# Six buffers for gathered rows in a mixture-of-experts decoder layer, with the projection weights split later

## What is computed

```python
logits = einsum('bsd,de->bse', x, router_w) + router_b
topk_vals, topk_idx = top_k(logits, 2)
topk_w = softmax(topk_vals)
h = einsum('td,edf->etf', x, expert_w) + expert_b
combined = sum over the two experts of topk_w * silu(h)
out = combined @ proj_w + proj_b
y = x + out
x = layernorm(x + norm_w * y / sqrt(mean(y*y) + eps))
```

## Time and profile before

| | |
|---|---|
| median of 3 runs | 1613.41 us (1609.93 to 1615.18) |
| profiled execution | 1619.38 us, span 1617.6 us |
| PE busy | 1476.6 us, 91% |
| DVE, ACT, POOL busy | 963.2, 654.9, 647.8 us |
| mean granted TensorE clock | 0.961 |
| end of cross attention, start of the expert stage's matmuls | about 1394 and 1419 us from the span's start |
| last expert matmul, last instruction | about 1532 and 1617 us |

### The profile page before, as it was taken

How to read it: one execution, slowest core, us unless ns; L and a number is a source line. 1 busy time by engine, 2 the same in 40 slices (tenths; PEclk the granted TensorE clock), 3 DMA queues, 4 the chain that set the end, 5 groups by cost and what they waited for, 6 DMA issues and landing times. The chain is left out here.

```text
span 1617.6 us, 27685 instructions
## 1 busy us (share of the span) xinstructions
PE 1476.6 (91%) x8462; PEld 1208.2 (75%) x8462; DVE 963.2 (60%) x3585; ACT 654.9 (40%) x1763; POOL 647.8 (40%) x1003
## 2 busy tenths in 40 slices
PE   6999999999997589999999999999999999389876
PEld 6777877878865377888888888878888888277754
DVE  3666566566665375566655665556555665744467
ACT  4434344343341263444444443444444446333344
POOL 1334334234232254344444444343443444354173
PEclk8999999999998789999999999999999999789988
DMA  6221221221211532111111212111121113565472
GB/s 204 103 73 61 91 71 61 91 71 61 92 61 52 175 121 69 52 60 58 42 59 54 63 39 62 59 54 53 42 67 50 61 47 109 195 171 158 136 224 82
DMA packets 60957, 139.75 MB, mean 86 GB/s; under 512 B 10182, under 2 KB 21034, under 8 KB 59876
## 3 DMA queue, kind: packets, MB, share of 16 engines
q1 hardware_dynamic: 56296, 123.85, 23.1%
q0 software_dynamic: 4576, 14.95, 3.6%
HBM read 94.31 MB, written 44.46 MB: 86 GB/s over the span
## 5 line engine op out<-in xcount | busy, mean ns | idle before, releaser
L932 ACT ACTIVATE b_probs<-b_probs,b_nmax 100x361 f32<-100x361 f32 x256 | 152.0, 594 | 71.3 <-DVE b_nmax L1037 71.0
L67 PE MATMUL b_bank<-b_kTh,b_q 128*100 128x362 f32 x512 | 174.0, 341 | 3.6 <-DVE b_kTl L1019 1.7
L1176 POOL TENSOR_TENSOR b_pcarry<-b_half 128x1 f32<-128x1 f32 x176 | 41.5, 236 | 323.4 <-DVE b_rinv L1043 267.4
L1037 DVE CUSTOM_DVE_ANT_0 b_probs<-b_bank,b_mask 100x361 f32<-100x361 f32 x256 | 135.5, 529 | 56.3 <-issue 46.6
L1201 POOL TENSOR_SCALAR b_probs<-b_probs,b_rinv 100x361 f32<-100x361 f32 x256 | 157.3, 626 | 0.0
L1030 DVE TENSOR_TENSOR b_pTl<-b_bank,b_pTh 121x400 fp32r<-121x400 f32 x192 | 110.0, 573 | 52.6 <-ACT b_pTh L927 52.6
L927 ACT ACTIVATE b_pTh<-b_bank 121x400 fp32r<-121x400 f32 x192 | 96.8, 504 | 101.1 <-PE b_bank L773 98.9
L975 ACT ACTIVATE b_oTh<-b_bank,b_bv 128x400 fp32r<-128x400 f32 x64 | 38.0, 594 | 207.1 <-PE b_bank L67 207.1
L773 PE MATMUL b_bank<-b_ident,b_probs 100*121 100x100 f32 x768 | 110.5, 266 | 5.7 <-POOL b_probs L1201 5.7
L773 PEld LDWEIGHTS b_bank<-b_ident,b_probs 100*121 100x121 f32 x768 | 108.1, 187 | 8.1 <-POOL b_probs L1201 7.2
L67 PE MATMUL b_bank<-b_Woh,b_oTh 128*100 128x512 f32 x256 | 108.2, 423 | 2.6 <-DVE b_oTl L1104 2.6
(11 more groups left out here) (251 smaller groups left out, 3967.6 us busy)
## 6 DMA issues: line engine op xcount, KB each, us to landing
q_d<-a_qo SPq DMA_DIRECT2D x64, 400.0 KB, 2.4
b_q<-q_d SPq DMA_DIRECT2D x64, 400.0 KB, 3.1
b_ctxr<-in_ctxT SPq DMA_DIRECT2D x48, 242.0 KB, 3.8
y_d<-c_y SPq DMA_DIRECT2D x32, 256.0 KB, 3.6
c_Eraw<-in_expert_w SPq DMA_DIRECT2D x10, 512.0 KB, 12.1
a_stage<-in_Wq SPq DMA_DIRECT2D x4, 1024.0 KB, 5.9
stage<-in_Wo SPq DMA_DIRECT2D x8, 512.0 KB, 3.7
a_xTr<-in_xT SPq DMA_DIRECT2D x8, 400.0 KB, 3.2
```

Source lines behind the costliest of these rows:

```text
L67: mm = eng.matmul(out, lhsT=l(c), rhs=r(c), start=first and k == 0, stop=last and k == n - 1)
L932: act.activation(p, p, ACT.Exp, scale=-1.0, bias=nmax[:, s % 2, h:h + 1], accum_out=psums[:, s % 2, h:h + 1]).then_inc(e_rdy, 1)
L1037: dve.tensor_tensor_reduce(out=probs[:, s % 2, h, 0:SE], in0=s_bank[h % 2][0:S, 0:SE], in1=mask_s[:], scale=-1.0, scalar=BIG, op0=ALU.add, ...
L1176: pool.tensor_tensor(pcarry[:, k:k + 1], half_s[:, 0:1], half_s[:, 0:1], ALU.add)
```

## The change

- `xg` gets six buffers instead of three; `x2a` becomes a view of the last three of them. Gather j waits for the transposes of tile j-6.
- The load of `x2a` moves from the middle of SP's list to behind the last store of y, with a wait for all transposes.
- SP waits for `gt_done` of 6 (tile 5 transposed) before it loads the projection weights, instead of for the second gather.
- POOL issues six gathers before its first two splits; the next three splits stand behind gathers 6 to 8, the projection's behind gathers 16 and 17. ACT's part of the projection split moves from tile 7 to tile 12.
- In the last batch of cross attention, `expert_hi` comes after `oTh` instead of before it.

The size of SBUF in use stays the same.

```diff
--- before.py
+++ after.py
@@ -45,6 +45,7 @@
 NT = 13
 NJ = 32
 PRE = 3
+NG = 3
 ROUTE_WIDTHS = (S, P, NJ, E * E, NT, B)
 ROUTE_COLS = sum(ROUTE_WIDTHS)
 ROUTE_SPANS = [(sum(ROUTE_WIDTHS[:k]), sum(ROUTE_WIDTHS[:k + 1])) for k in range(len(ROUTE_WIDTHS))]
@@ -966,14 +967,14 @@
                     if first:
                         for k in range(2):
                             split_hi(KV_PIECES + 2 * s + k)
-                    if last and s >= 2:
-                        for m in range(PRE * (s - 2), PRE * (s - 1)):
-                            expert_hi(m)
                     if before:
                         kv = (s + 3) % 4
                         act.wait_ge(o_done, n)
                         act.activation(oTh[:, kv, :], o_bank[:, 0:XG * S], ACT.Identity,
                                        bias=bv_s[:, kv:kv + 1]).then_inc(o_hi, 1)
+                    if last and s >= 2:
+                        for m in range(PRE * (s - 2), PRE * (s - 1)):
+                            expert_hi(m)
                     if s == 0 and now and not first:
                         for c in range(KC):
                             values_hi(j, c)
@@ -1316,8 +1317,8 @@
         shift = [small[:, 4 + 5 * NT + t:5 + 5 * NT + t] for t in range(NT)]
         stat = sb("c_stat", [P, NT, 6])
         nw_s, pb_s, ones_s = stage[:, 0, 0], stage[0:1, 0, 1], stage[:, 1, 0, 0:P]
-        x2a = sb("c_x2a", [P, 3, D])
-        xg = sb("c_xg", [P, 3, D])
+        xg = sb("c_xg", [P, 2 * NG, D])
+        x2a = xg[:, NG:2 * NG]
         tok_s, tok_f = sb("c_tok", [P, NJ], U32), sb("c_tok_f", [P, NJ])
         pick_b, pick_s = sb("c_pick_b", [S, B, 4], U32), sb("c_pick", [P, NT, 4], U32)
         te_s, te_f = sb("c_te", [1, NJ], I32), sb("c_te_f", [1, NJ])
@@ -1363,7 +1364,7 @@
         route, exp_rdy, pick_rdy = sem("c_route"), sem("c_exp_rdy"), sem("c_pick_rdy")
         iota_set = sem("c_iota_set")
         cnt_done, q_rdy, tok_done, tok_set = sem("c_cnt_done"), sem("c_q_rdy"), sem("c_tok_done"), sem("c_tok_set")
-        xg_in, gt_done, g_hi, g_lo = [sem(f"c_xg_in{k}") for k in range(3)], sem("c_gt_done"), sem("c_g_hi"), sem("c_g_lo")
+        xg_in, gt_done, g_hi, g_lo = [sem(f"c_xg_in{k}") for k in range(2 * NG)], sem("c_gt_done"), sem("c_g_hi"), sem("c_g_lo")
         h_done, h_rdy, y_rdy, y_out = sem("c_h_done"), sem("c_h_rdy"), sem("c_y_rdy"), [sem("c_y_out0"), sem("c_y_out1")]
         r_in, r_w1, c_rdy = [sem(f"c_r_in{k}") for k in range(NT)], sem("c_r_w1"), sem("c_c_rdy")
         ct_done, c_hi, c_lo, p_done = sem("c_ct_done"), sem("c_c_hi"), sem("c_c_lo"), sem("c_p_done")
@@ -1394,7 +1395,7 @@
                     sp.dma_start(ident_s[:], ident).then_inc(ident_in, 16)
                     sp.dma_start(eb_s[:], expert_b.partition_broadcast(P)).then_inc(eb_in, 16)
                 if n == 2 * E:
-                    sp.wait_ge(xg_in[1], 16)
+                    sp.wait_ge(gt_done, 2 * NG)
                     sp.wait_ge(x2_out, 16 * B)
                 raw = pieces[n][1].rearrange("p (c d) -> p c d", c=2)
                 sp.dma_start(raw, pieces[n][0]).then_inc(w_raw[n], 16)
@@ -1402,7 +1403,6 @@
             sp.dma_start(pick_d.rearrange("(b s) c -> s b c", s=S), pick_b[:]).then_inc(pick_out, 16)
             sp.dma_start(pb_s, proj_b.rearrange("(a d) -> a d", a=1)).then_inc(tail_in, 16)
             sp.dma_start(nw_s, norm_w.partition_broadcast(P)).then_inc(tail_in, 16)
-            sp.dma_start(x2a[:], x2_f[0:3 * P, :].rearrange("(t p) d -> p t d", p=P)).then_inc(x2_in[0], 16)
             sp.wait_ge(pick_out, 16)
             full = (NT - 1) * P
             sp.dma_start(pick_s[:, 0:NT - 1], pick_d[0:full, :].rearrange("(t p) c -> p t c", p=P)).then_inc(pick_in, 16)
@@ -1410,6 +1410,8 @@
             for j in range(NJ):
                 sp.wait_ge(y_rdy, j + 1)
                 sp.dma_start(y_d[j * P:(j + 1) * P, :], y_s[:, j % 2]).then_inc(y_out[j % 2], 16)
+            sp.wait_ge(gt_done, NJ)
+            sp.dma_start(x2a, x2_f[0:3 * P, :].rearrange("(t p) d -> p t d", p=P)).then_inc(x2_in[0], 16)
             sp.wait_ge(r_w1, 1)
             for k in range(3):
                 sp.dma_start(x2b[:, 3 * k:3 * k + 3], x2_f[(3 + 3 * k) * P:(6 + 3 * k) * P, :].rearrange("(t p) d -> p t d", p=P)).then_inc(x2_in[k + 1], 16)
@@ -1438,9 +1440,9 @@
             pe.wait_ge(ident_in, 16)
 
             def transpose_slots(j):
-                pe.wait_ge(xg_in[j % 3], 16 * (j // 3 + 1))
+                pe.wait_ge(xg_in[j % (2 * NG)], 16 * (j // (2 * NG) + 1))
                 for c in range(DC):
-                    mm = pe.transpose(t_bank[j % 2][:, c * P:(c + 1) * P], xg[:, j % 3, c * P:(c + 1) * P], ident_s[:])
+                    mm = pe.transpose(t_bank[j % 2][:, c * P:(c + 1) * P], xg[:, j % (2 * NG), c * P:(c + 1) * P], ident_s[:])
                 mm.then_inc(gt_done, 1)
 
             def expert(j):
@@ -1512,7 +1514,7 @@
                 act.wait_ge(h_rdy, j + 1)
                 wait(act, y_out[j % 2], 16 * (j // 2))
                 act.activation(y_s[:, j % 2], h_s[:, j % 2], ACT.Silu).then_inc(y_rdy, 1)
-                if j == E - 1:
+                if j == E + 4:
                     split_hi(2 * E)
                     split_hi(2 * E + 1)
                     act.wait_ge(tail_in, 32)
@@ -1745,9 +1747,9 @@
                 pool.tensor_tensor(pieces[n][3], pieces[n][1], pieces[n][2].bitcast(F32), ALU.subtract).then_inc(w_lo[0], 1)
 
             def gather_slots(j):
-                wait(pool, gt_done, j - 2)
-                pool.indirect_dma_start(out=xg[:, j % 3], out_offset=None, in_=x2_f,
-                                        in_offset=bass.IndirectOffsetOnAxis(ap=tok_s[:, j:j + 1], axis=0)).then_inc(xg_in[j % 3], 16)
+                wait(pool, gt_done, j - 2 * NG + 1)
+                pool.indirect_dma_start(out=xg[:, j % (2 * NG)], out_offset=None, in_=x2_f,
+                                        in_offset=bass.IndirectOffsetOnAxis(ap=tok_s[:, j:j + 1], axis=0)).then_inc(xg_in[j % (2 * NG)], 16)
 
             pool.memset(ones_s, 1.0).then_inc(set_up, 1)
             pool.memset(half_s, -0.5).then_inc(set_up, 1)
@@ -1758,13 +1760,13 @@
             pool.wait_ge(tok_set, 1)
             for j in range(NJ):
                 gather_slots(j)
-                if j == 2:
+                if j == 2 * NG - 1:
                     split_lo(2 * PRE)
                     split_lo(2 * PRE + 2)
-                if PRE <= j < E - 2:
-                    split_lo(2 * j + 4)
-                if j in (E + 2, E + 3):
-                    split_lo(2 * E + j - E - 2)
+                if 2 * NG <= j < 2 * NG + E - PRE - 2:
+                    split_lo(2 * (j - 2 * NG) + 4 + 2 * PRE)
+                if j in (2 * E, 2 * E + 1):
+                    split_lo(j)
 
             def gather_results(t):
                 n = rows(t)
```

## The result

The changed kernel takes **1631.49 us** (median of 4 runs, 1628.92 to 1633.11), beside 1614.3 us for the kernel before (4 runs, 1609.93 to 1617.56): a ratio of **1.010 [1.008, 1.012]**, slower by 17 us. The profiled execution took 1628.92 us, the lowest of its four, with a span of 1627.1 us.

What follows compares the result with a forecast made beforehand. The prediction took PE to bound the expert stage except where it waits. Terms 10.7 + 2.6 - 0.6 + 0.5 + 1.0 gave +14.2 us on 1613.4, so 1627.6 us, range 1619 to 1634.5.

Steps and rivals of the forecast that it cites:

- The sign: Whole kernel: the change makes it slower, chance 0.93; same 0.04, faster 0.03.
- the mechanism: Expert stage: SP's new wait delays y's store 0, so ACT, then DVE, then tile 4's matmuls on PE wait.
- the swap: Cross attention, last batch: oTh before expert_hi delays the next slot's first pTh; +1.0 us, between -0.5 and +2.9.
- the stand: PE idle from tile 5's transposes (T5) to tile 4's matmuls (E4): 16.3 us, net +10.7 after 5.7 regained.
- the low clock: Expert stage, behind PE's long idle time: PE comes back at the lower clock level, +2.6 us.
- The short passage: Rival: SP's queue, wake to store 0's landing, takes 7.6 us on less loaded DMA engines; 1620.9 us, chance 0.22.
- The 5.7 us regained at T3: Tile 3's transposes: six buffers remove the 2.99 us wait for rows and 2.76 us of low clock; -5.7 us.
- the step that called the POOL splits covered by 3 us: Early expert stage: POOL's two splits end by 1426.9, some 3 us before tile 3's matmuls first need them.
- mid-stage: Middle of expert stage: gathers no longer wait behind POOL's two splits; -0.6 us, between 0 and -1.2.
- tail: Expert stage's end: the residual load ahead of the result gathers delays them; +0.5 us, between 0 and +3.4.
- the rival "faster": Tile 4's matmuls: no stall comes and the gains stay; 1607.8 us, deciding passage 2.7 us or less, chance 0.03.

Runs made afterwards that it cites:

- e6_wait_only: The kernel before with only SP's new wait (tile 5 transposed), three row buffers and the rest as before: 1636.33 us, 1.0133.
- e4_lists_first: The changed kernel with pick list's store and loads, bias and norm row ahead of SP's wait, only two weight loads behind it: 1629.74 us, 1.0090.
- e1_old_wait: The changed kernel with SP waiting for the second gather's landing again, all else kept: 1618.55 us, 1.0014.
- e2_old_order: The changed kernel with expert_hi ahead of oTh again in cross attention's last batch: 1634.33 us, 1.0119.
- e5_wait_4: The changed kernel with SP waiting for the transposes of tile 3 instead of tile 5: 1628.47 us, 1.0087.
- e7_weights_behind_y: The changed kernel with pick list, bias, norm row early, projection weight loads behind y stores 5 and 7, expert_hi before oTh: 1614.81 us, 0.9996.
- e14_after_row: The changed kernel with DVE's weight splits at tiles 3 to 5 behind the rows' low part, POOL's five in a row behind gather 5: 1632.66 us, 1.0106.
- e3_swap_only: The kernel before with only oTh put ahead of expert_hi in the last batch: 1617.05 us, 1.0019.
- e9_dve_late: e7_weights_behind_y with DVE's three weight splits moved from tiles 0 to 2 to tiles 3 to 5, behind the rows' low part: 1614.05 us, 1.0001.

## Why the prediction was right, and where not

**The sign, the mechanism and the range** held: 1631.5 us lies in 1619 to 1634.5, 3.9 above the 1627.6 forecast. That the trace's difference, 13.9 us, is so near the sum of 14.2 is in part luck: the swap was taken 1.6 too low, the stand and the low clock together 1.8 too high. The experiments on SP's wait carry the mechanism from both sides: without the wait 1.0014, with it alone 1.0133.

**The stand before E4.** Forecast 16.3, measured 14.76. Wake and passage were each a little long: 1434.0 against 1432.76, some of which is only that the execution was earlier (T5 began at 1433.3 by the forecast, at 1432.13 by the trace), and 14.2 us to the landing against 12.7. The forecast moved SP's slow issues along with the queue and was right in that: the bias issue took 3.88 us (3.17 before) and the pick list's store 7.8 us until SP could go on (6.7 before), although no residual load went beside it. What I took too long is the end: without the residual load ahead of them, the second pick load's issue took 1.27 us instead of 4.35 (3.13 in e6_wait_only, which still has that load there) and store 0 landed in 2.3 instead of 4.1.

**The short passage** (7.6 us) didn't come. Its condition, DMA engines less loaded, wasn't met: from 1433.6 to 1441.4 their mean busy share was 1.00, with the two weight loads and four gathers that POOL issued from 1431.90 to 1437.91. Whether the issue behind the pick store would be quick on idle DMA engines no run shows; it took 2.18 us in e4_lists_first, at a share of 0.81. The Trainium skill's fit for one transfer (DMA: Bandwidth & Descriptors, "Anatomy of one DMA"), made for DMAs that GpSimd issues, would give an estimate of about 2.1 us for the pick store. The traces are far from it for this store of 1,600 pieces of 16 bytes, issued by SP: 7.8 us in the changed kernel, and 5.05 in e4_lists_first (1408.62 to 1413.67), where the projection weight loads weren't ahead of it.

**The 5.7 us regained at T3** came in the profiled execution (T0 to T5 17.27 against 22.49), but the reason was only half of it. I gave the gain to the buffers; they are enough (e1_old_wait), but so is moving the traffic with three (e6_wait_only), and the changed kernel does both. And the step that called the POOL splits covered by 3 us looked at the experts that need them, not at DVE: in four of the six kernels profiled with the changed order of the splits (e1_old_wait, e2_old_order, e5_wait_4, e7_weights_behind_y) DVE's first split was held up by POOL's pair, T0 to T5 took 20.5 to 21.0 us, and some 1.5 to 2.0 of the 5.2 us were left of the gain. This is the term that the sum lacked; with a split of "up to 2.69 us" I had bounded it by the row of before, and it went to 6.19 in e1_old_wait and 6.23 in e5_wait_4.

**The swap** was mis-sized: +1.0 forecast, +2.6 in the trace (-2.3 undone, +3.9 alone), within the bound of 2.9 for the first two and above it alone. ACT's rows show why it lost: oTh, now first, waited 2.32 us idle for PE, time that the copies had filled before, and came only 0.45 us sooner behind the origin, while the first pTh, now behind the copies' 2.94 us, came 2.41 us later.

**Low clock, mid-stage and tail** came out as +1.7, -0.6 and +0.4, for +2.6, -0.6 and +0.5. The first results' wait at the end is 7.56 us, 7.54 before: the residual load hides in the gap.

**What stays open.** The two profiles differ by 13.9 us behind the origin, the medians by 17.2. DVE meeting POOL would add 3.6 us in other executions of the changed kernel, and I took that for the answer, but e14_after_row has it removed and is no faster. Its trace shows +14.4 us behind the origin and its median +17.9. In every kernel with a stand the median's difference is the larger (e6_wait_only: 21.4 against 18.1), in those without one the two agree within 2.1 us. One execution of each is profiled, so what the others do in those 1 to 6 us isn't shown. A part may be the clock behind the wait at E14 (E9 with the old place of ACT's split): that tile period took 5.27 to 5.32 us in seven traces, the changed kernel's among them, and 6.40 to 6.84 in five (e1_old_wait, e3_swap_only, e4_lists_first, e5_wait_4, e6_wait_only), each with a mean grant of 0.72 over the six microseconds around it instead of 1.00. PE had stopped for the same 1.8 us in all twelve; what decides isn't shown. That the median of e4_lists_first fell so little belongs to the same gap. A smaller slip of the prediction changes nothing here: its own numbers put the edge of the rival "faster" at a passage of 3.6 us (1439.44 less 1434.0 and 1.84), not 2.7. A wait for a later tile than T5 was not tried: by the order of the code T6 follows E4, E4 the Silu of tile 2 and that the store of y, so SP would wait for itself.

## What to carry to other kernels

Before you add a wait to an in-order queue, list what stands behind it there and follow each of those to who waits for it; here a wait meant to keep loads out of the gathers' way held a store, the store held a buffer, and the buffer held the matmuls. Loads without a hurry go behind the urgent small ones, each behind something that comes at a known pace, so that the wait that they need is already met (gt_done of 6 behind the stores of y 5 and 7, from e7_weights_behind_y on). When work on DVE and POOL reads SBUF with two inputs each, keep the two apart in time, or count for DVE what is left of POOL's work on top of its own; starting DVE up to 0.62 us earlier did not save it.

## What was not expected of the hardware

- DVE's 128x1024 subtraction with both inputs in SBUF takes 1.22 us alone, 3.24 when it starts just behind one such operation of POOL, and 5.7 to 6.2 with two. It ends 1.08 to 1.11 us behind POOL's, in every trace where it is held up. DVE was spared in two traces, where it started 0.67 and 0.70 us before POOL (the changed kernel and e4_lists_first), and paid when it was 0.62 us or less ahead (e6_wait_only), or behind. POOL gives up little in turn (4.68 to 4.72 us for two against 4.67, 5.08 to 5.12 where DVE was spared).
- A store of 25 KB in pieces of 16 bytes took from 4.89 us (e9_dve_late) to 9.35 (e1_old_wait) until the queue could go on, and the issue right behind it took 1.80 us in the first and 5.53 in the second. The DMA engines were busy meanwhile, with mean shares of 0.92 and 0.78 (1.00 in the changed kernel).
- A gather of 128 rows took 9.1 us to land among large loads and 3.9 without them. What looked like a shortage of row buffers was that.
- After one and the same stop of 1.8 us PE came back at full clock in seven traces and at a mean grant of 0.72 in five.
